# One read of a projection's bank by ScalarE, first bf16 parts made by GpSimd, and attention maxima stored with four heads side by side

## The reference

```python
h = _layernorm(x) * (1 + ca) + sa
x = x + ga * attention(h)          # 16 heads of 16 features
h = _layernorm(x) * (1 + cb) + sb
x = x + gb * ffn(h)                # square(relu(h @ W_fc.T)) @ W_proj.T, then 5 steps that count spikes

def attention(h):
    q, k, v = ...                                         # projections with bias
    s = einsum('bhqd,bhkd->bhqk', q, k) / sqrt(16)
    p = softmax over each window of 128 keys, causal      # zero where a window is all masked
    p = softmax(p, axis=-1)                               # again, over all 1024 keys
    return (p @ v) @ Wo.T + bo
```

## Time and profile before

| | |
|---|---|
| time, median of 3 runs | 2343.7 us (2340.61 to 2345.05) |
| profiled execution | 2340.14 us, span 2338.3 us |
| mean granted clock of TensorE | 0.992 |
| busy: TensorE, VectorE, ScalarE, GpSimd | 93%, 75%, 66%, 49% |
| chain that ended last | TensorE 79%, VectorE 12%, ScalarE 5% |

### The profile page before, as it was taken

How to read it: one execution, slowest core, us unless ns; L and a number is a source line. 1 busy time by engine, 2 the same in 40 slices (tenths; PEclk the granted TensorE clock), 3 DMA queues, 4 the chain that set the end, 5 groups by cost and what they waited for, 6 DMA issues and landing times.

```text
span 2338.3 us, 47111 instructions
## 1 busy us (share of the span) xinstructions
PE 2184.4 (93%) x19388; PEld 1242.1 (53%) x19388; DVE 1748.5 (75%) x2115; ACT 1541.8 (66%) x2157; POOL 1137.6 (49%) x1070
## 2 busy tenths in 40 slices
PE   6889889999999999999998999999999999989998
PEld 4444344465555555455554655545555565545567
DVE  7887888768787676886778777786877767788466
ACT  2577677766667667676777766776667766667741
POOL 3153133545664456644676257663576544443540
PEclk9999999999999999999999999999999999999999
DMA  5233122211122113121133102231022211101000
GB/s 188 64 116 89 48 62 75 84 48 39 53 64 84 53 35 91 49 61 53 35 91 95 50 18 60 66 109 48 9 70 78 84 31 51 33 21 32 7 28 25
DMA packets 114066, 140.25 MB, mean 60 GB/s; under 512 B 8648, under 2 KB 86760, under 8 KB 113856
## 3 DMA queue, kind: packets, MB, share of 16 engines
q1 hardware_dynamic: 113856, 137.24, 20.7%
HBM read 74.28 MB, written 58.74 MB: 57 GB/s over the span
## 4 chain that ended last, share of the span: by engine, by line
PE 79%; DVE 12%; ACT 5%; issue 2%; DMA 1%; SPq 0%; ACTq 0%
PE pv L822 11%; PE sums L812 9%; PE score L797 9%; PE score L742 9%; PE ring L772 9%; PE sums L754 9%; DVE e L1205 5%; PE score L691 5%; PE score L706 4%; DVE negmax L1183 4%; PE ring L851 4%; PE score L800 2%; PE ring L775 2%; PE score L682 2%; ACT e L1066 2%
## 5 line engine op out<-in xcount | busy, mean ns | idle before, releaser
L1066 ACT ACTIVATE e<-score 128x512 f32<-128x512 f32 x1152 | 672.0, 595 | 374.2 <-PE score L800 202.3
L1205 DVE TENSOR_TENSOR e<-ring,e 128x1024 f32<-128x1024 f32 x576 | 681.3, 1224 | 276.3 <-PE ring L851 275.8
L1183 DVE TENSOR_REDUCE negmax<-ring 128x8 f32<-128x1024 f32 x576 | 681.4, 1220 | 138.2 <-PE ring L775 127.4
L1071 ACT ACTIVATE e<-e 128x2048 f32<-128x2048 f32 x288 | 548.8, 1906 | 4.1 <-DVE e L1205 4.1
L797 PE MATMUL score<-q_st,k_st 112*128 112x512 bf16 (+3 forms) x1536 | 458.8, 330 | 56.8 <-ACT e L1066 21.9
L772 PE MATMUL ring<-k_st,q_st 96*128 96x512 bf16 (+3 forms) x1664 | 387.7, 318 | 46.3 <-DVE e L1205 24.1
L1514 POOL TENSOR_SCALAR r_p<-r_b,ab 128x256 bf16<-128x256 f32 x96 | 89.6, 934 | 539.0 <-DVE r_b L1211 539.0
L822 PE MATMUL pv<-e,v 128*17 128x512 f32 (+3 forms) x3072 | 312.7, 494 | 1.3 <-DVE o_t L1223 1.3
L812 PE MATMUL sums<-e,d_ones 128*32 128x256 f32 x4608 | 304.6, 383 | 1.3
L797 PEld LDWEIGHTS score<-q_st,k_st 112*128 112x128 bf16 x1536 | 147.6, 97 | 246.5 <-issue 119.5
L1493 POOL TENSOR_TENSOR gT<-gT 128x512 f32<-128x512 f32 x112 | 117.2, 1050 | 326.0 <-ACT gT L1039 326.0
(11 more groups left out here) (148 smaller groups left out, 2544.4 us busy)
## 6 DMA issues: line engine op xcount, KB each, us to landing
q_st<-q_parts SPq DMA_DIRECT2D x31, 768.0 KB, 6.0
k_st<-k_parts SPq DMA_DIRECT2D x31, 768.0 KB, 8.7
q_parts<-qk_p SPq DMA_DIRECT2D x30, 384.0 KB, 2.6
k_parts<-qk_p SPq DMA_DIRECT2D x28, 384.0 KB, 2.6
x_in<-in_x SPq DMA_DIRECT2D x8, 1024.0 KB, 5.6
q_parts<-qk_p SPq DMA_DIRECT2D x30, 256.0 KB, 2.9
x_res<-in_x SPq DMA_DIRECT2D x30, 256.0 KB, 4.5
k_parts<-qk_p SPq DMA_DIRECT2D x28, 256.0 KB, 2.9
```

The costliest lines, as they stand in the source:

```text
L1066: act.activation(e[:, n % ES, hh, :], score[SCORE_SLOT["st", n, hh][0]][:, :], ACT.Exp, scale=DK ** -0.5).then_inc(e1_done, 1)
L1071: act.activation(v, v, ACT.Exp).then_inc(e2_done, 1)
L1183: dve.tensor_reduce(negmax[:, hh:hh + heads, at:at + NB // heads], slot[:, :].rearrange("p (h a n) -> p h a n", h=heads, n=P), AX_X, ALU.m ...
L1205: dve.tensor_tensor(v, ring[no % 2][:, :].rearrange("p (i n) -> p i n", i=2), v, ALU.mult).then_inc(ring_free, 1)
```

## The change

1. ScalarE reads the bank of a `QK` piece once, for batches after the first: it writes `qk_f` and releases the bank. It still waits for `split_lo`, no longer for `stored`.
2. GpSimd waits for `stored`, copies `qk_f` rounded to bf16 into the first part (a fourth operation, with a semaphore `split_hi` of its own), and makes the other two parts as before.
3. `negmax` is laid out by window with the four heads side by side, so the reduction writes its eight values 16 bytes apart for one head; the cast and the subtraction of the split go through windows and then heads, instead of heads and then windows.
4. `placed(n)` has four places, one after each head; pieces at (n, 1) get the key (n, 3), and the engines' steps and `score_slots` walk the four heads in a loop.

```diff
 def placed(n):
-    out = [None, None]
+    out = [None] * QH
...
-        negmax = sb("negmax", [P, QH, SLOTS])
+        negmax = sb("negmax", [P, SLOTS, QH])
...
@@ ScalarE, take
                     if no >= 8:
+
                         act.wait_ge(split_lo, no - 1)
-                        act.wait_ge(stored[no % 2], 48 * (no // 2))
+                        act.activation(whole_of(no), ps, ACT.Identity, bias=b_qk[:, t, ot:ot + 1]).then_inc(piece_evac, 1)
+                        return
                     act.activation(whole_of(no), ps, ACT.Identity, bias=b_qk[:, t, ot:ot + 1])
                     act.activation(parts_of(no)[:, 0, :], ps, ACT.Identity, bias=b_qk[:, t, ot:ot + 1]).then_inc(piece_evac, 1)
...
@@ VectorE, maxima and split_maxima
-                dve.tensor_reduce(negmax[:, hh:hh + heads, at:at + NB // heads], slot[:, :].rearrange("p (h a n) -> p h a n", h=heads, n=P), AX_X,
+                dve.tensor_reduce(negmax[:, at:at + NB // heads, hh:hh + heads].rearrange("p w h -> p h w"), slot[:, :].rearrange("p (h a n) -> p h a n", h=heads, n=P), AX_X,
                                   ALU.max, negate=True).then_inc(ring_free, 1)
...
-                hi, lo = (maxp[:, own, a, :].rearrange("p w h -> p h w") for a in range(2))
+                hi, lo = (maxp[:, own, a, :] for a in range(2))
...
-                dve.tensor_copy(hi, negmax[:, :, own]).then_inc(max_hi, 1)
+                dve.tensor_copy(hi, negmax[:, own, :]).then_inc(max_hi, 1)
                 dve.wait_ge(max_hi, no + 1)
-                dve.tensor_tensor(lo, negmax[:, :, own], hi, ALU.subtract).then_inc(max_lo, 1)
+                dve.tensor_tensor(lo, negmax[:, own, :], hi, ALU.subtract).then_inc(max_lo, 1)
...
@@ GpSimd, finish
                     piece_done(pool, *item)
+                    if no >= 8:
+                        pool.wait_ge(stored[no % 2], 48 * (no // 2))
+                        pool.tensor_copy(p3[:, 0, :], f).then_inc(split_hi, 1)
+                        pool.wait_ge(split_hi, no - 7)
                     pool.tensor_tensor(p3[:, 1, :], f, p3[:, 0, :], ALU.subtract).then_inc(split_mid, 1)
```

More of the change, by code:

```diff
@@ L106 @@
 FIRST[26, 0] = ("BH", 1, 0)
[L107 removed]
+FIRST[26, 3] = ("BT", 1, 0)
 def backs(n):
@@ L901, in step @@
             def step(n):
-                first, second = placed(n)
+                p = placed(n)
                 single = quanta(n)
@@ L915, in step @@
                     one_over_sums(n - LAG_R, 1)
-                if piece_first(n) and first:
-                    piece(first)
+                if piece_first(n) and p[0]:
+                    piece(p[0])
                 if mixed(n):
@@ L921, in step @@
                     maxima(*at[-1])
[L922 to L953, removed]
+                for hh in range(QH):
+                    if n < NUNIT:
+                        scores(n, hh)
+                    if hh == 3 and 2 in at:
+                        maxima(*at[2])
+                    if p[hh] and not (hh == 0 and piece_first(n)):
+                        piece(p[hh])
+                    if hh == 1 and turns(n) and not late_turn(n):
+                        turn_maxima(*turns(n))
+                    tile = {1: 0, 2: 1, 3: 3}.get(hh)
+                    if tile in at:
+                        maxima(*at[tile])
+                    if hh == 3 and turned_out(n):
+                        outputs(*turned_out(n))
+                    for item in single[hh]:
+                        quantum(n, *item)
                 if late_turn(n):
@@ L1111, in step @@
                     sum_exp(t)
[L1112 to L1121, removed]
-                if turns(n) and not late_turn(n):
-                    take_turned(*turns(n))
-                for item in sums_ended(n, 1):
-                    take_sum(*item)
-                if n < NUNIT:
-                    first_exp(n, 2)
-                for item in sums_ended(n, 2):
-                    take_sum(*item)
-                if n < NUNIT:
-                    first_exp(n, 3)
-                if second:
-                    take(second)
-                for item in sums_ended(n, 3):
-                    take_sum(*item)
+                if piece_first(n) and p[0]:
+                    take(p[0])
+                for hh in range(QH):
+                    if n < NUNIT:
+                        first_exp(n, hh)
+                    if p[hh] and not (hh == 0 and piece_first(n)):
+                        take(p[hh])
+                    if hh == 1 and turns(n) and not late_turn(n):
+                        take_turned(*turns(n))
+                    for item in sums_ended(n, hh):
+                        take_sum(*item)
                 if late_turn(n):
@@ L1408, in step @@
                     invert(t)
-                first, second = placed(n)
-                if first and first[0] == "O":
-                    take_output(first)
+                p = placed(n)
+                for item in p[:2]:
+                    if item and item[0] == "O":
+                        take_output(item)
                 tiles = tiles_of(n)
@@ L1414, in step @@
                     maxima(g, k)
-                if second and second[0] == "O":
-                    take_output(second)
+                for item in p[2:]:
+                    if item and item[0] == "O":
+                        take_output(item)
                 if turned_out(n):
```

22 lines of the change are left out of this document (11 added, 11 removed).

## The result

The changed kernel takes 2334.0 us (median of 7 runs, 2327.3 to 2338.0) against 2345.0 us for the kernel before (7 runs, 2340.6 to 2347.4): ratio 0.995, interval 0.9934 to 0.9966. Faster, as forecast, but by 11 us where 29 were forecast. That it lies inside the stated range of 2303 to 2335 us, by 1 us, is no support for the sum: the range reached so far for the sake of the rivals (a) and (b), and neither is what happened in a steady batch. The profiled execution took 2336.3 us (span 2334.5).

A forecast was written before the change was run, and what follows sets the result against it. TensorE was taken as the bound, busy 2184.4 of 2338.3 us, with waits to win. One bank read (15.0) plus the maxima layout (14.0) gave 29 us off the median 2343.7: 2315 us, range 2303 to 2335.

The forecast's parts named there:

- (a): Rival: the split of the maxima stays as dear, mixed types being the cost and not distance; 2329 us, 12%.
- (b): Rival: TensorE gets ahead and waits at the ring instead, losing half the gain; 2329 us, 13%.
- the price of the split: VectorE's cast and subtraction of the maxima: 0.35 us each in the new layout, from 0.61 and 0.92.
- edit 3: GpSimd makes the first part: 56 copies of 0.6 us, 34 us more GpSimd work, priced at nothing.
- the cover of 3.8 us: Time between GpSimd's tightest split of the inverses and TensorE's reading it, against up to 0.5 us delay.
- (d): Rival: slower, GpSimd becomes late; costs once its chain ends over 3.8 us later; 2358 us at 10 late, 3%.
- 0.58 + 0.25 + 0.22 + 0.68 + 1.46 + 0.61 = 3.8 us: Gain in each of six later batches: four shortened bank-read waits (1.73), then two waits for the maxima (1.46, 0.61).
- the 1.46 of the turn: Cast and subtraction before 982.27 go from 2.88 to 1.42 us, taking 1.46 of TensorE's 1.52 us wait.
- 4.6 + 1.5 = 6.1 us: Gain outside the six later batches: 4.6 from bank-read waits; from maxima waits, excesses of 0.48, 0.30 and 0.76.
- (c): Rival: more goes than the listed waits, half of TensorE's 21.9 us for exponentials; 2305 us, 10%.
- (e): Rival: it does nothing, other waits ending at the same moment replace the old one for one; 2342 us, 4%.
- the signs that were to show me wrong: Batch shrinks under 2 us; waits for lines 1205 and 1183 grow over 10 us; or `r_p` releases TensorE.

The follow-up runs named there:

- e2_read_only: Kernel before with one read of the bank by ScalarE and GpSimd's copy, old layout of the maxima: 2339.0 us, ratio 0.9975.
- e1_maxima_only: Kernel before with the new layout of negmax and the new split alone; ScalarE still reads each bank twice: 2339.4 us, ratio 0.9981.
- e3_way_norm: Changed kernel, with GpSimd waiting at step 17 of a batch until VectorE's four normalisation tiles are done: 2322.0 us, ratio 0.9905 to the kernel before.
- e9_before_way: Kernel before with only GpSimd's wait at step 17 for VectorE's four normalised tiles added: 2342.5 us, ratio 1.0.
- e5_after_again: Changed kernel once more, unaltered, timed beside the kernel before: 2330.9 us, ratio 0.9945.
- e6_scalar_copies: Changed kernel, but ScalarE makes the rounded first part from qk_f after releasing the bank, so GpSimd keeps three operations: 2335.9 us, ratio 0.9961 to the kernel before.
- e7_two_copies: Changed kernel with a second GpSimd copy, later overwritten, in each chain: 2348.4 us, ratio 1.0017 to the kernel before.
- the probes: Changed kernel with four extra VectorE operations of 168 elements behind each split of the maxima, to measure prices only: run once, 2340.0 us, not compared.
- e4_way_both: As e3_way_norm, with GpSimd also waiting at step 15 until VectorE has split the maxima: 2322.0 us, ratio 0.9903 to the kernel before.

## Why the prediction was right and wrong

**Right.** The direction, and the price of the split: 0.25 and 0.33 us undisturbed for 0.35 and 0.35. Line 1014's waits went, with 0.44 us left of the 1.02 (0.34 forecast). The reduction stayed at 1.217 us with its values 16 bytes apart, so no price for that. GpSimd's copy 0.61 us for 0.6. Step order cost nothing that shows.

**The step that failed** is "I price edit 3 at nothing". The argument asked who reads what GpSimd *makes* (`r_p`, the squares, the stores), and there the cover of 3.8 us held. It didn't ask what VectorE does while GpSimd works. Some rows were there: the earlier trace rows show that a GpSimd subtraction lengthens VectorE's, and the prediction used it for the split and as rival (d), with its price only beyond 3.8 us of delay. The chain didn't come late, it came early: the 0.58 us of bank time saved put GpSimd's chain at the start of four tiles instead of behind the first two, and a fourth operation gave each of them a partner. Four tiles went from 3.15 to 4.38 us, and TensorE, no longer held by the read, was there to feel it: 1.53 us in each of six batches, 9.2 us. e2_read_only has it, e1_maxima_only has it not, e3_way_norm takes it away, e9_before_way shows that it wasn't there before.

The Trainium skill describes this (SBUF — State Buffer, Who interferes with whom, and the section SBUF: two separate sides): VectorE and GpSimd share one pair of ports as an exclusive lock that is held for a whole instruction, so that the other blocks and doesn't run slower; VectorE has a pair of its own besides, and takes the shared one only in a 2-port mode or when an instruction has two inputs in SBUF and GpSimd's reads SBUF. The trace agrees that an operation waits for its partner's end and isn't stretched by a factor: each met tile ends 0.15 us after its partner, 0.67 us long beside 0.61 and 1.32 beside 1.16, against 0.41 alone. In the kernel before, the subtraction of 0.91 us that began at 980.50 ended 0.76 us after GpSimd's of 980.15 had the earlier trace rows: it had most of its own work still to do. The trace agrees too that not every operation is held up. The layer norm's statistics read and write SBUF, and stay at 0.41 us beside a GpSimd operation (changed kernel; two of them, overlapping):

```profile
978.05 1.16 POOL L1461 TENSOR_TENSOR qk_f<-qk_f,qk_p 128x512 f32<-128x512 f32 x1
978.09 0.74 DVE L1130 BATCH_NORM_STATS2 ln_stats<-x_res 128x6 f32<-128x256 f32 x2
```

Whether the tiles and the cast ran in a 2-port mode no row shows. Nor does the record say what counts as being first: the second to fourth tile of the changed kernel begin 0.01 us ahead of their partners and wait for them.

**Terms that were mis-sized.** A steady batch was to give 0.58 + 0.25 + 0.22 + 0.68 + 1.46 + 0.61 = 3.8 us. It gave 0.58 where 0.68 stood (1.02 less 0.44): ScalarE's two reads overlap. In the kernel before the second begins 0.1 us ahead of the first one's end, so a bank comes free 0.58 us sooner and not by the whole 0.68 of line 1014:

```profile
986.57 0.69 ACT L1013 ACTIVATE qk_f<-score,b_qk 128x512 f32<-128x512 f32 x1 [1.43 <-PE score L706]
987.15 0.68 ACT L1014 ACTIVATE qk_p<-score,b_qk 128x512 bf16<-128x512 f32 x1
```

It gave 0.92 (1.52 less 0.60) for the 1.46 of the turn: I had kept one GpSimd addition of 0.72 us over 0.70, 1.42 in all, but both operations have a partner, 0.68 + 1.28 = 1.96. That is 0.10 and 0.54 less; with 1.53 for the tiles 3.80 − 2.17 = 1.63, and 1.58 was measured.

The beginning was to give 4.6 + 1.5 = 6.1 us and gave 2.3 at most. From the first product of the first unit to the first of unit 37 it took 245.9 us before, 243.5 in e5_after_again, and 246.9 in the profiled execution of the same changed kernel; the granted clock of these stretches was 0.98, 0.99 and 0.97. How much of that is the change's and how much the clock's isn't separated. Rival (b) was right there. TensorE in time, the changed kernel:

```profile
131.62 0.22 PE L772 MATMUL ring<-k_st,q_st 96*128 96x128 bf16 x1 [2.38 <-DMA k_st<-k_parts]
...
149.72 0.60 PE L772 MATMUL ring<-k_st,q_st 96*128 96x512 bf16 x2 [0.44 <-DVE negmax L1156]
```

and in the kernel before, where the row of 151.23 and two more like it follow that of the earlier trace rows:

```profile
151.23 0.39 PE L797 MATMUL score<-q_st,k_st 112*128 112x512 bf16 x1 [0.58 <-ACT qk_p L1014]
```

What TensorE won at the first turns it gave back at 131.62 for a load of `k_st` that hadn't landed. Every profiled kernel with a part of the change waits there (1.1 to 2.9 us, e2_read_only 1.4), and the kernel before and e9_before_way don't. Over the whole span such waits grew from 5.2 us to 7.2, and to 8.5 in e5_after_again; the sum has no term for them, and why the load is late isn't shown; e1_maxima_only, which leaves GpSimd's part as it was, has it too. Of each 0.58 TensorE gave back 0.21 to 0.44 at the ring. The sum 29 − 6 × 2.2 − 3.8 = 12 us, with the 2.3 of e5_after_again for the beginning, stands beside 11 us measured, and 13.6 in e5_after_again against the kernel before beside it.

**The clock.** The prediction didn't have TensorE's granted clock, and equal programs differ by it. The seven runs of the changed kernel go with its mean: 2327.3 us at 0.993, 2328.8 at 0.992, 2334.0 at 0.99, 2336.3 at 0.989, 2338.0 at 0.988, some 2 us for each 0.001; of the other two, 2334.8 was at 0.99 and 2330.0 at 0.993. Inside one execution it shows as well: the changed kernel's batch from 1452 to 1734 us took 281.07 us where the one before it took 278.4, and TensorE's clock was 0.52 from 1552 to 1559, with TensorE busy for 6.78 of these 7 us. In e9_before_way the batch from 1180 to 1462 took 281.72 and not 280.03, with a clock of 0.63 from 1268 to 1272. The profiled execution of the changed kernel is one of low clock. In it and in e5_after_again, the same stretch near the beginning reads (columns: length, TensorE's busy time, clock, DMA share, GB/s):

```profile
60.00:340.00 280.00, 242.27 (x2365) 0.97 0.25 73
```

```profile
60.00:340.00 280.00, 241.01 (x2393) 0.99 0.27 76
```

The kernel before shows 0.98 there. e1_maxima_only, e6_scalar_copies and e7_two_copies had lower mean clocks than the kernel before (0.990, 0.990, 0.988), e3_way_norm and e9_before_way had not. Why the clock falls where it does is open; no run changed it alone. By the 2 us for each 0.001 it is worth 2 to 4 us between the medians here, an estimate.

**The rivals.** (a) is refuted by the probes. (b) held in the first batch; in the steady one (880 to 1160 us) TensorE's waits for the ring grew by 0.39 us only, from 2.64 to 3.03. Those for exponentials grew too, by 0.33, so (c) is false. All waits of over 0.1 us there add up to 10.66 us before and 9.07 after, which is the batch's 1.58. (d) named the right engine and the right resource with the wrong condition: GpSimd early, not late. (e) is what e4_way_both met at the turn. Of the signs that were to show me wrong, one came: the batch shrank by 1.58, less than 2 us.

With GpSimd giving way the batch gives 3.15 us, and 29 − 6 × 0.65 − 3.8 = 21 us are left; 22 were measured. That version, e3_way_norm, beats both kernels by one wait.

## What to carry to other kernels

When work is moved to GpSimd or released earlier, list what VectorE does in the stretch where GpSimd will now run, not only who waits for GpSimd's results. In this case the operations to ask about are those with two inputs in SBUF, and the casts and scalings from SBUF to SBUF; each that stands beside a GpSimd operation must be priced to that one's end, and with what it has left to do after that. Operations that read one input from PSUM, reductions and the norm's statistics took their usual time beside GpSimd. Where GpSimd has slack, one wait that lets it begin behind VectorE's urgent tiles can be worth more than the edit itself (9 us here, against 4.5 for the one read alone), but only once TensorE arrives early enough to feel them. Sum a steady batch, check it against the profile of one batch, and treat the beginning as a place of its own.

## What the hardware showed that was not expected

- Some VectorE operations that GpSimd meets end shortly after GpSimd's: the cast of the split took 0.68 us beside 0.61 and the subtraction 1.28 beside 1.16, 0.25 and 0.33 being their time alone. A longer one ends later: the subtraction of the kernel before, 0.91 us alone, ended 0.76 us behind its partner. The reduction that reads `ring`, a PSUM tile, keeps its 1.212 to 1.227 us in all 576 cases, and the norm's statistics, from SBUF to SBUF, their 0.41. GpSimd's subtractions of 512 columns take 1.16 us, and 1.21 to 1.26 where they begin inside such an operation (980.15, 981.44, 993.18 in the kernel before).
- The tiles feel the number of GpSimd operations they meet: the four together took 1.38, 3.15 and 4.38 us with none, the last two and all four met.
- GpSimd's copy from fp32 to bf16 of 512 columns costs 0.61 us, its two-input subtraction of the same size 1.16.
- Runs of the same program lie 8 to 11 us apart (six and seven runs of the changed kernel), in step with their mean granted clock, so that a change of under 0.3% needs the clock of each run beside its time.
